# GNN forward pass on one core: in the second node pass the out product becomes feature-major, and its GELU is summed with h2 in PSUM and added by VectorE

## The reference

```
h = relu(layernorm(x))
r = relu(h @ W_res + b_res);  agg = edge softmax of h[src].h[dst], applied to h[src] @ W_conv, summed by dst
x = x + batchnorm(agg + r)
h2 = relu(layernorm(x))
m = gelu(gelu([h2[src], h2[dst], edge_attr] @ W_m1 + b_m1) @ W_m2 + b_m2)
boxes = m summed by dst
x = x + h2 + gelu(gelu([h2, boxes] @ W_c1 + b_c1) @ W_c2 + b_c2)
```

## Time and profile before

| | us |
|---|---|
| median of 3 runs (1946.9 to 1965.65) | 1961.68 |
| profiled execution: its span | 1753.3 |
| what lies around the span (the median less the span) | 208.4 |
| busy PE, DVE, ACT, POOL in the span | 1375.6, 1361.7, 833.2, 1363.7 |
| mean granted clock of TensorE (share of 2.4 GHz) | 0.831 |

### The profile page before, as it was taken

The page is one execution under the profiler, slowest core; times in us unless marked ns, Lnnn a source line. Parts: engine busy times, 40 slices in busy tenths (PEclk is TensorE's granted clock), DMA queues, the critical chain, the costliest instruction groups (busy, mean ns, idle before and its releaser), DMA issues.

```text
span 1753.3 us, 21724 instructions
## 1 busy us (share of the span) xinstructions
PE 1375.6 (78%) x6521; PEld 942.1 (54%) x6521; DVE 1361.7 (78%) x2229; ACT 833.2 (48%) x1448; POOL 1363.7 (78%) x1135
## 2 busy tenths in 40 slices
PE   3487777777776776988999889858889988787993
PEld 1266666666555564766667666634445444343541
DVE  8899899989877858898889888825767766555871
ACT  4655455545543435776668666621333432332441
POOL 7777777778777778788888887675767768888676
PEclk9788889888887877898889888955888987886987
DMA  7788776545543363444545565545656554545520
GB/s 210 249 283 290 282 264 219 165 145 157 161 150 96 106 224 102 157 166 166 201 162 186 174 200 178 160 98 108 121 120 124 118 117 97 107 89 98 122 48 18
DMA packets 154342, 273.55 MB, mean 156 GB/s; under 512 B 58386, under 2 KB 69361, under 8 KB 154228
## 3 DMA queue, kind: packets, MB, share of 16 engines
q1 hardware_dynamic: 71144, 183.91, 31.1%
q0 software_dynamic: 68112, 49.85, 16.7%
q10 hardware_dynamic: 14972, 38.41, 5.9%
HBM read 151.68 MB, written 121.80 MB: 156 GB/s over the span
## 4 chain that ended last, share of the span: by engine, by line
POOL 40%; issue 20%; DVE 18%; PE 13%; DMA 6%; ACT 2%; SPq 0%; POOLq 0%; DVEq 0%; ACTq 0%
POOL agg_rows L591 11%; POOL out L591 10%; POOL agg_ring L587 7%; DVE stat L756 4%; POOL xt L637 3%; DVE stat L764 3%; POOL part L587 3%; DMA rr<-edge_x 3%; DMA edge_agg<-agg_ring 2%; POOL rr L631 2%; DVE xc L770 1%; PE banks L1350 1%; DVE sums L821 1%; PE banks L1542 1%; PE banks L1540 1%
## 5 line engine op out<-in xcount | busy, mean ns | idle before, releaser
L587 POOL DMA_INDIRECT agg_ring<-agg_rows,edge_idx x196 | 233.2, 1190 | 112.2 <-DMA edge_agg<-agg_ring 57.2
L591 POOL DMA_INDIRECT agg_rows<-agg,put_first x196 | 234.0, 1194 | 55.9 <-issue 54.7
L587 POOL DMA_INDIRECT part<-in_x,edge_idx x192 | 217.3, 1132 | 58.5 <-issue 58.2
L591 POOL DMA_INDIRECT out<-agg,put_last x196 | 212.0, 1082 | 59.6 <-issue 59.6
L1335 PE MATMUL banks<-ident,xc 128*128 128x128 f32 (+1 forms) x784 | 135.1, 322 | 141.6 <-DVE xc L770 140.9
L1466 PEld LDWEIGHTS banks<-packed,cT 97*128 97x128 f32 (+1 forms) x1568 | 210.4, 218 | 45.3 <-issue 44.3
L1466 PE MATMUL banks<-packed,cT 97*128 97x64 f32 (+1 forms) x1568 | 218.6, 303 | 0.5 <-ACT cT L1198 0.5
L1335 PEld LDWEIGHTS banks<-ident,xc 128*128 128x128 f32 (+1 forms) x784 | 113.3, 177 | 152.0 <-DVE xc L770 130.8
L1456 PE MATMUL banks<-hT,packed 64*96 64x512 f32 (+1 forms) x392 | 125.5, 718 | 47.6 <-ACT cT L1198 43.0
L1081 ACT ACTIVATE hT<-banks 128x512 f32<-128x512 f32 (+1 forms) x98 | 55.4, 595 | 205.7 <-PE banks L1335 204.3
L587 POOL DMA_INDIRECT x_ring<-in_x,edge_idx x104 | 121.4, 1167 | 34.2 <-issue 34.2
(11 more groups left out here) (163 smaller groups left out, 3351.2 us busy)
## 6 DMA issues: line engine op xcount, KB each, us to landing
xt<-in_x SPq DMA_DIRECT2D x84, 512.0 KB, 5.2
r_rows<-rT ACTq DMA_DIRECT2D x48, 512.0 KB, 5.4
agg_rows<-rb SPq DMA_DIRECT2D x48, 512.0 KB
out<-xt SPq DMA_DIRECT2D x36, 512.0 KB, 3.0
edge_r<-rr ACTq DMA_DIRECT2D x48, 256.0 KB, 5.0
rT<-r_rows SPq DMA_DIRECT2D x24, 512.0 KB, 6.5
part<-r_rows SPq DMA_DIRECT2D x24, 512.0 KB, 6.9
rr<-edge_r SPq DMA_DIRECT2D x48, 256.0 KB, 3.2
```

Source lines behind the costliest of these rows:

```text
L587: A.indirect_dma_start(to, None, table[:, :], bass.IndirectOffsetOnAxis(ap=idx, axis=0), bounds_check=limit, oob_is_err=False).then_inc(si ...
L591: A.indirect_dma_start(table[:, :], bass.IndirectOffsetOnAxis(ap=idx, axis=0), rows_of, None, bounds_check=limit, oob_is_err=False).then_i ...
```

## The change

- **Out product** (`out_product`): W_c2 is stationary, c moves, 512 columns at a time, two matmuls per half instead of eight; the result has features on partitions. One bank (6) holds both halves in turn, so the product of one half waits until the GELU of the half before has read it. The bias goes into the GELU (`gelu_out`); the row of ones in cT goes.
- **sum_back** is new on TensorE: for each half, four matmuls with h2T as the stationary operand and the identity as the moving one, and four with the GELU's output, accumulate in bank 7. That turns both back into rows and sums them. It waits for `final_half` of the half before.
- **VectorE** adds that bank to x2, 512 columns at a time (`final_half`, two per step instead of one `final_rows`). The second half of an even step is added at the end of the round, behind the inversion and both L770; `final_rows` of that step stood ahead of them. `add_h2` and its semaphore go from GpSimd.
- h2T gets four slots (half steps) instead of two, as it is read twice.
- **Orders**: TensorE, with p and q the steps of the pair before and r the q of the round before, does: transpose p0, out r1, c p0, back r0, transpose p1, transpose_r b, out p0, c p1, back r1, transpose q0, out p1, c q0, back p0, transpose q1, out q0, c q1, back p1, transpose_r a + 2. ScalarE: gelu_c r1, gelu_out r0, copy p0, norm_r b, gelu_c p0, gelu_out r1, copy p1, square a, gelu_c p1, gelu_out p0, copy q0, square b, gelu_c q0, gelu_out p1, copy q1, norm_r a + 2.
- **GpSimd**: `put_agg` of the 31 groups that are left runs in one row, then all 49 `gather_agg`, then stage 3. The ring has 8 slots (`RS`; four of them in gout[1]), and SyncE stashes by `agg_gathered`: 1.6 groups per step, 41 by the last step, the rest in stage 3. `put_final` begins at g = 10, one group per group.

```diff
 XS = 6
 CS = 3
-RS = 4
+RS = 8
+HS = 4
 GS = 8
 XB = 8
 RB = 4
+AGG_PACE = 1.6
 LEAD = 3
 FIRST_PUT = 30
...
         esq = [sb(f"esq{q}", [P, EC]) for q in range(2)]
+        h2T = [hT[:, 0:HALF], hT[:, HALF:2 * HALF], esq[0][:, :], esq[1][:, :]]
+        goT = [gout[0][:, 0:HALF], gout[0][:, HALF:2 * HALF]]
...
 
-        def agg_groups(s):
-            return PUTS_AHEAD + s + 1 + (s + 1) // 6
+        def agg_gathered(s):
+            return max(0, min(G, int(AGG_PACE * s) - (G - PUTS_AHEAD) - 4))
+
+        def half_of(s, b):
+            return 2 * s + b
...
                         load_rows(s)
-                due = min(G, max(stashed, agg_groups(min(a - 2, S - 1)) - G))
+                due = max(stashed, agg_gathered(a - 2))
...
                         do(g)
-                due = max(stashed, min(G, agg_groups(S - 1) - G + a + 3))
+                due = min(G, stashed + 4)
...
-            def add_h2(s):
-                p = nodes_of(s)
-                pool.wait_ge(B_h.sem, B_h.after(s))
-                here = xb[s % XB][0:p, :]
-                A.tensor_tensor(here, here, xc[s % CS][0:p, :], ALU.add).then_inc(B_y.sem, 1)
-
             def put_final(g):
...
-            for s in range(S):
-                add_h2(s)
-                for n in range(agg_groups(s - 1), agg_groups(s)):
-                    if is_group(n):
-                        put_agg(n)
-                    if n == G:
-                        G_p.all_done(pool, G)
-                    if is_group(n - G):
-                        gather_agg(n - G)
-            ahead = agg_groups(S - 1) - G
-            last = G - ahead
+            for n in range(PUTS_AHEAD, G):
+                put_agg(n)
+            G_p.all_done(pool, G)
+            pool.wait_ge(s_same, 32)
+            for g in range(G):
+                gather_agg(g)
             put = 0
...
                     add_agg(g + 2)
                 add_x(g)
-                if is_group(g + ahead):
-                    gather_agg(g + ahead)
-                if g == last:
+                if g == 0:
                     B_st.all_done(pool, S)
-                due = min(g - 9, 2 * (g - last))
-                while put < due:
+                if g >= 10:
                     put_final(put)
                     put += 1
...
                 subtract_mean(xc[s % CS][0:p, :], here, dstat(0, s, p), B_f, s, 2)
 
-            def final_rows(s):
-                p = nodes_of(s)
-                here = xb[s % XB][0:p, :]
-                dve.wait_ge(B_og.sem, B_og.after(s))
-                dve.wait_ge(B_y.sem, B_y.after(s))
-                V.tensor_tensor(here, here, gout[s % 2][0:p, :], ALU.add).then_inc(B_fin.sem, 1)
+            def final_half(s, b):
+                p = nodes_of(s)
+                here = xb[s % XB][0:p, b * HALF:(b + 1) * HALF]
+                dve.wait_ge(B_bk.sem, B_bk.after(s, b + 1))
+                dve.wait_ge(B_f.sem, B_f.after(s))
+                V.tensor_tensor(here, here, bank(7)[0:p, :], ALU.add).then_inc(B_fin.sem, 1)
 
             for i in range(PAIRS + 2):
...
                 if is_step(a - 3):
-                    final_rows(a - 3)
+                    final_half(a - 3, 0)
                 if b in pair:
                     x2_center(b)
+                if is_step(a - 3):
+                    final_half(a - 3, 1)
                 if a in pair:
                     p = nodes_of(a)
                     sum_squares(dstat(1, a, p), sq[0][0:p, :], B_sq, a, B_ss)
                 if b in pair:
                     sum_squares(dstat(1, b, P), sq[1][:, :], B_sq, b, B_ss)
                 if is_step(a - 2):
-                    final_rows(a - 2)
+                    final_half(a - 2, 0)
                 if pair:
                     invert(i, nodes_of(pair[-1]), 0, R * len(pair), B_inv, B_ss, pair[-1])
                 for s in pair:
                     p = nodes_of(s)
                     t_ = rows(xc[s % CS][0:p, :])
                     relu_scale(t_, t_, dstat(3, s, p), B_h)
+                if is_step(a - 2):
+                    final_half(a - 2, 1)
                 if i == 1:
...
             def gelu_out(s, b):
                 p = nodes_of(s)
-                c = slice(b * HALF, (b + 1) * HALF)
                 act.wait_ge(B_o.sem, B_o.after(s, b + 1))
-                B_fin.done(act, s - 2)
-                A.activation(gout[s % 2][0:p, c], bank(6 + b)[0:p, :], ACT.Gelu).then_inc(B_og.sem, 1)
+                B_bk.part(act, s - 1, b + 1)
+                if s == 0 and b == 0:
+                    act.wait_ge(E_ctr.sem, E_ctr.after(G - 1))
+                    X_st.all_done(act, G)
+                A.activation(blocks(goT[b], p), blocks(bank(6), p), ACT.Gelu, bias=bc2[:, :]).then_inc(B_og.sem, 1)
 
             def copy_h2T(s, b):
                 p = nodes_of(s)
-                c = slice(b * HALF, (b + 1) * HALF)
                 act.wait_ge(B_t.sem, B_t.after(s, b + 1))
-                B_c.part(act, s - 1, b + 1)
-                A.activation(blocks(hT[:, c], p), blocks(W[1][:, c], p), ACT.Copy).then_inc(B_ht.sem, 1)
+                B_bk.part(act, s - 2, b + 1)
+                if s == 1:
+                    act.wait_ge(E_ss.sem, E_ss.after(G - 1))
+                A.activation(blocks(h2T[half_of(s, b) % HS], p), blocks(W[1][:, b * HALF:(b + 1) * HALF], p), ACT.Copy)\
+                 .then_inc(B_ht.sem, 1)
 
...
+                                   blocks(h2T[half_of(s, b) % HS][i * D:i * D + D, :], p), start=True, stop=True)
                 ins.then_inc(B_c.sem, 1)
 
             def out_product(s, b):
                 p = nodes_of(s)
-                to = bank(6 + b)
                 pe.wait_ge(B_cg.sem, B_cg.after(s, b + 1))
-                B_og.part(pe, s - 1, b + 1)
-                for i in range(8):
-                    ins = T.matmul(to[0:p, i * D:i * D + D], cT[b][:, i % 2, (i // 2) * P:(i // 2) * P + p],
-                                   wc2[:, :], start=(i == 0), stop=(i == 7))
+                if b:
+                    pe.wait_ge(B_og.sem, B_og.after(s, 1))
+                else:
+                    B_og.done(pe, s - 1)
+                for i in range(2):
+                    ins = T.matmul(blocks(bank(6)[i * D:i * D + D, :], p), wc2[:, :], blocks(cT[b][:, i, :], p),
+                                   start=True, stop=True)
                 ins.then_inc(B_o.sem, 1)
 
+            def sum_back(s, b):
+                p = nodes_of(s)
+                pe.wait_ge(B_ht.sem, B_ht.after(s, b + 1))
+                if b:
+                    pe.wait_ge(B_fin.sem, B_fin.after(s, 1))
+                else:
+                    B_fin.done(pe, s - 1)
+                for k in range(4):
+                    T.matmul(bank(7)[0:p, k * P:(k + 1) * P], h2T[half_of(s, b) % HS][:, k * P:k * P + p], ident[:, :],
+                             start=(k == 0), stop=False)
+                pe.wait_ge(B_og.sem, B_og.after(s, b + 1))
+                for k in range(4):
+                    ins = T.matmul(bank(7)[0:p, k * P:(k + 1) * P], goT[b][:, k * P:k * P + p], ident[:, :],
+                                   start=False, stop=(k == 3))
...
```

90 lines of the change are left out of this document (52 added, 38 removed).

## The result

The changed kernel took 2118.8 us (median of 5, 2106.3 to 2121.0), the kernel before beside it 1961.7 (median of 5, 1942.1 to 1970.8). The ratio is 1.080, with a 95% interval of 1.073 to 1.087: 8% slower, where 3% faster was forecast.

A forecast was written before the change was run, and what follows sets the result against it. GpSimd was taken to set the pace. Stage 2 +17 us, between stages +20, groups 0 to 48 -93 and end -10 gave -65: 1961.7 - 65 = about 1896 us, range 1840 to 1950.

The forecast's parts named there:

- span plus 208.4 outside, which the change doesn't touch: Whole kernel: the median time is the profiled span plus 208.4 us outside it, so 1961.7 - 65 gives about 1896.
- Cost: nothing, hidden behind TensorE: GpSimd in stage 2: 444 us of puts and gathers fit in the stage's 525 us, so they add nothing.
- the gap: Between stages 2 and 3, last addition to first sum_edges: 38 us against 18 before, 20 us lost.
- the end: After the last sum of stage 3: remaining final scatters take 44 us against 53.6 before, -10.
- the one on the slower side: Stage 3 held by its loads-to-sum path, not GpSimd's list: 22.4 us per pair, 2011 us in all, chance 0.06.
- the rule on weight loads: TensorE's sum_back: a skill text's rule implied 160 ns per record instead of 111, a pair 3.1 us longer.
- That rival: TensorE in stage 2: weight loads don't hide in sum_back, 22.6 us per pair, 1954 us in all, chance 0.03.
- The clock rival: TensorE keeps its earlier granted clock of 0.87 in stage 2: 22.4 us per pair, 1949 us, chance 0.12.
- the stretch of rows 9: Stage 3 before, from group 38 on: 17.9 us per pair, used as measure for changed stage 3 and full-clock evidence.
- The loop over the loads of x: Stage 2: a loop through store, load and VectorE's round takes 18.5 us, close beside TensorE's 19.5 per pair.
- the floor of 16.6: TensorE in stage 3: 16.6 us per pair at least, with 17.6 taken for the forecast.
- both floors are reached: Stage 2 at 19.0 us per pair, stage 3 at 16.6, 30 us between them: 1835 us, chance 0.12.

The follow-up runs named there:

- b0_before_again: The kernel before, run again without an edit: 1949.4 us, ratio 1.003.
- a0_again: The changed kernel, run again without an edit beside a kernel before of 1746.6 us: 1649.6 us, ratio 0.946.
- v2_puts_after_stage1_c: The changed kernel with its row of 31 puts held back until stage 1 has ended: 2124.1 us, 1.078 of the kernel before.
- v15: The changed kernel with puts and gathers paced by stage 2's steps, plus one 1.0 us fill behind each group of four DMAs: 1823.9 us, ratio 0.935.
- v12: The changed kernel with three fills (3.0 us) behind each group in its rows of puts and gathers of agg: 1837.1 us, ratio 1.054.
- v13: As v12, plus one fill behind every four gathers of x and every early group of puts in stage 1: 1924.4 us, ratio 1.103.
- v6: The changed kernel with each put of the row and each gather of agg waiting for the group before: 1822.2 us, ratio 1.045.
- v7: The changed kernel with at most four gathers of x under way in stage 1: 1866.2 us, ratio 1.070.

## Why the prediction was wrong

**The step that failed first: "span plus 208.4 outside, which the change doesn't touch".** I had a span of 1753.3 and times near 1962 and explained the difference with time outside the span. It was a disagreement between two conditions, and it sat in stage 1, where GpSimd's gathers of x come in unbroken rows (b0_before_again: 2 us outside). Taken seriously, it would have asked what costs 200 us on the timed chip and not in the profile, and whether the change makes more of it.

**The step that decided: GpSimd's row "Cost: nothing, hidden behind TensorE".** It counted the time of the row, 444 us against 525, and was right on that. It took for granted that an engine which only issues DMAs leaves the others alone. In the held condition it doesn't: TensorE's signals come up to 88 us late beside the unbroken row. Against before of the held set (b0_before_again), by the table: stage 1 ends 153 us later; the stretch from there to the last addition takes 604 us, not 502, +102; the gap +23; stage 3 -107; the end -1. Together +171 (rounded terms), which is 2104.3 - 1933.4. No rival had this place; the one on the slower side was stage 3, which came out fastest. The range, too, was made of stages 2 and 3 alone.

**What was right, as the free condition shows** (a0_again, against the span of 1688 forecast and 1642.7 measured):
- TensorE: four records of out product 1.01 us (forecast 1.08), the sixteen of sum_back 1.00 + 0.89 = 1.89 (1.78), and a half with its transposes repeats every 4.46 us:

```profile
769.73 1.10 PE L1461 MATMUL banks<-hT,packed 64*96 64x512 f32 x4
770.76 1.16 PE L1485 MATMUL banks<-ident,esq 128*128 128x128 f32 x8
771.76 1.06 PE L1489 MATMUL banks<-ident,gout 128*128 128x128 f32 x8
772.65 0.60 PE L1340 MATMUL banks<-ident,xc 128*128 128x128 f32 x4
773.18 1.08 PE L1473 MATMUL banks<-cT,packed 96*64 96x512 f32 x4
774.19 1.10 PE L1461 MATMUL banks<-esq,packed 64*96 64x512 f32 x4
```

- Weight loads did hide, about: 0.118 us per record, and the 0.16 of the rule on weight loads that the prediction weighed isn't seen. That rival falls. The clock rival falls too: 1.00 in every window from 700 to 1150 us. One support of it was misread all the same: the stretch of rows 9 did not run at the full clock without a break, it has 0.50 from 1610 to 1620 us and 0.51 from 1680 to 1690.
- Stage 2: 464.4 us for 24 pairs, 19.35 each, not 20.2. The loop over the loads of x cost nothing: -21.
- The drain from the last x2_center 32 us instead of 39, and stage 1 8 us shorter than on the page.
- VectorE: the halved addition 0.686 us, forecast 0.69.
- The gap: 39.0 us from the end of the last addition (39.7 from its start, as in the table), forecast 38.
- Stage 3: 403.7 us, 16.8 per pair, close to the floor of 16.6, not 17.6: -18.
- The end: 52 us behind the last sum, not 44. 44 scatters (eleven groups) stood behind the last `add_x`, not 40, and took 1576.4 to 1637.5, 61 us in place of 55.

These make 1643 instead of 1688. The rival "both floors are reached" came nearest in the stages (19.35 and 16.8 us per pair, for its 19.0 and 16.6), though its shorter gap did not come; 5.4% faster is what the change is worth where nothing is held up.

**Open.** What makes a set held or free was not found: the same number of chip (7) came up in both kinds, and whether these were one device I can't tell. How GpSimd's row reaches TensorE is open too. It isn't the moving of data: the DMA engines are 8% busy in the windows of the stop. VectorE and ScalarE are not held by themselves: their own signals come at once, and each of their long waits read above ends on TensorE or on the other of the two. SyncE isn't held either: in the moved row of v2_puts_after_stage1_c its two loads of r are issued in 0.43 and 0.32 us, 33.6 us apart, the second behind ScalarE's `norm_r`.

A rival that no run tests is the recording. The held traces have only about half of the semaphore events of the free ones, and every run here, timed ones too, comes with a span and a granted clock of its own, so none is known to have run unrecorded. Whether the stop would be there without the recording is not shown.

What a break has to be is known in part. An addition of 2.4 us, fills of 3.0 or 1.0 us, and in stage 3 the two accumulating DMAs of `add_agg` and `add_x` behind every four scatters all serve: with these last, GpSimd busy for 41 of 50 us, none of TensorE's 261 recorded signals between the first and the last sum_edges is over 1 us late. Not tried were an idle gap of 1 us, and a row without breaks at a slower pace, so that the break and the lower rate of indirect DMAs (four per 6.2 us in v15, per 5.1 us in the row) aren't told apart; nor v12, v13, v6 and v7 in a held set.
